# Where the projections of the second layer stand among the attention tiles: four single products, or one block of four and one of two

## The reference

```python
# layer 0
xm = rmsnorm(x) * (1 + scale) + shift          # scale, shift = cond @ w_cond
q, k, v = split(xm @ w_qkv); q, k = rope(q), rope(k)
x = softmax(q k^T / 4) v @ w_out + x
# layer 1
xn = layer_norm(x)
q, k, v = xn @ q_w + q_b, xn @ k_w + k_b, xn @ v_w + v_b
y = softmax(q k^T + mask) v                    # over the keys, no scale
h = layer_norm(y) * (1 + scale) + shift        # scale, shift = silu(cond) @ emb_w + emb_b
x = x + silu(h) @ out_w + out_b
```

## Time and profile before

| | before |
|---|---|
| median of 3 runs | 534.52 us (533.82 to 536.47) |
| the profiled execution: its time / its span | 534.85 / 533.1 us |
| mean granted TensorE clock | 0.994 |
| busy: TensorE matmul / VectorE / ScalarE / POOL | 97% / 78% / 66% / 40% |
| instructions | 9837 |

### The profile page before, as it was taken

One profiled execution on the slowest core, in us unless ns is written; L12 is line 12 of the kernel. 1 busy time (PEld: TensorE's weight loads), 2 busy tenths in 40 slices (PEclk: granted clock), 3 DMA queues, 4 the chain that ended last, 5 costly groups with the idle time before them and its releaser, 6 DMA issues.

```text
span 533.1 us, 9837 instructions
## 1 busy us (share of the span) xinstructions
PE 516.3 (97%) x3342; PEld 195.3 (37%) x3342; DVE 413.7 (78%) x1073; ACT 350.0 (66%) x683; POOL 213.4 (40%) x223
## 2 busy tenths in 40 slices
PE   9978889999999999999999999999999999999987
PEld 5633323243443334332443334332433332332234
DVE  4776588789788678967789677977899998999126
ACT  1542455667767676776768676777788768677961
POOL 3169999238232321823235312723552044004401
PEclk8989999999999999999999999999999999999999
DMA  7982204144134133210331123310331112211011
GB/s 241 344 285 60 81 2 120 40 122 123 39 119 121 41 105 89 86 41 2 119 121 42 40 91 92 99 39 3 120 119 49 54 40 77 67 42 41 2 39 41
DMA packets 43033, 45.25 MB, mean 85 GB/s; under 512 B 4436, under 2 KB 41572, under 8 KB 42600
## 3 DMA queue, kind: packets, MB, share of 16 engines
q1 hardware_dynamic: 42696, 42.79, 26.0%
q10 hardware_dynamic: 288, 1.84, 0.9%
HBM read 25.46 MB, written 18.87 MB: 83 GB/s over the span
## 4 chain that ended last, share of the span: by engine, by line
PE 77%; DVE 14%; DMA 3%; issue 3%; ACT 2%; SPq 1%; DVEq 0%; ACTq 0%
PE bank L502 20%; PE bank L485 13%; PE bank L548 10%; PE bank L465 9%; PE bank L476 9%; DVE masked L818 6%; PE bank L559 5%; PE bank L576 4%; DVE row_max L821 4%; PE bank L517 3%; DMA X<-in_x 3%; PE bank L537 2%; ACT probs L671 1%; PE bank L584 1%; PE bank L615 1%
## 5 line engine op out<-in xcount | busy, mean ns | idle before, releaser
L671 ACT ACTIVATE probs<-bank 128x512 f32<-128x512 f32 x512 | 274.5, 598 | 90.1 <-PE bank L476 89.6
L821 DVE TENSOR_REDUCE row_max<-bank 128x1 f32<-128x512 f32 x256 | 162.6, 684 | 42.0 <-PE bank L485 40.9
L485 PE MATMUL bank<-k_s,q_s 64*128 64x512 f16 x512 | 188.9, 382 | 5.1 <-DVE row_max L821 4.2
L818 DVE CUSTOM_DVE_ANT_0 masked<-bank,mask_bias 128x512 bf16<-128x512 f32 x256 | 163.1, 687 | 18.1 <-PE bank L485 17.5
L465 PE MATMUL bank<-q_s,k_s 64*128 64x512 f16 x512 | 153.2, 381 | 1.1 <-ACT probs L671 0.6
L476 PE MATMUL bank<-shift,kx 64*128 64x512 f16 x512 | 148.5, 376 | 0.9 <-DMA shift<-shift_rows 0.9
L502 PE MATMUL bank<-probs,v_aug 128*17 128x512 f32 x1024 | 134.8, 598 | 0.7 <-ACT probs L671 0.7
L485 PEld LDWEIGHTS bank<-k_s,q_s 64*128 64x128 f16 x512 | 46.9, 93 | 155.0 <-DVE row_max L821 68.0
L548 PE MATMUL bank<-xT,wqkv 128*128 128x512 f32 x128 | 63.5, 628 | 2.8 <-ACT xT L696 2.8
L476 PEld LDWEIGHTS bank<-shift,kx 64*128 64x128 f16 x512 | 45.6, 95 | 28.9 <-DMA shift<-shift_rows 1.4
L465 PEld LDWEIGHTS bank<-q_s,k_s 64*128 64x128 f16 x512 | 31.1, 94 | 15.0 <-ACT probs L671 10.5
(11 more groups left out here) (108 smaller groups left out, 501.9 us busy)
## 6 DMA issues: line engine op xcount, KB each, us to landing
q_parts<-parts SPq DMA_DIRECT2D x64, 128.0 KB
k_parts<-parts SPq DMA_DIRECT2D x64, 128.0 KB
q_s<-q_parts SPq DMA_DIRECT2D x32, 256.0 KB, 2.8
k_s<-k_parts SPq DMA_DIRECT2D x32, 256.0 KB, 3.1
X<-in_x SPq DMA_DIRECT2D x4, 512.0 KB, 7.3
y<-X SPq DMA_DIRECT2D x7, 256.0 KB, 2.2
wc<-in_w_cond ACTq DMA_DIRECT2D x1, 1024.0 KB, 4.9
tables<-in_tables SPq DMA_DIRECT2D x4, 256.0 KB, 7.0
```

Source lines behind the costliest of these rows:

```text
L485: nc.tensor.matmul(bank, m.q_s[slot][rows, i, queries], m.k_s[slot][rows, i, :], start=True, stop=True).then_inc(q.d_made, 1)
L671: act.activation(m.probs[k][:, h, :], bank, ACT.Exp, scale=1.0 if s >= B * NG else float(DH) ** -0.5)\
L818: dve.tensor_tensor_reduce(m.masked[D["max", n, k, h] % ND][:, :], bank, m.mask_bias[:, b, :], 1.0, LOWEST, ALU.add, ALU.max, to)\
L821: dve.tensor_reduce(to, bank, AX.X, ALU.max).then_inc(q.d_done, 1)
```

## The change

The table `PIECES` is changed, and with it the order of POOL's program. The four query and key products of a second-layer batch stand behind tile k = 2 of group 7 + 4b, all four in a row; k = 1 and 3 of that group and k = 0 of the next are left empty. Both value products of a batch stand in a row behind k = 3 of the group where only the second was (9 + 4b, and group 20 for the last batch); the last batch of layer 0 goes the same way, from groups 4 and 5 to group 5. On POOL both value biases of batch b - 1 are added ahead of the splits of batch b, and the one behind the splits is gone; for the last batch both come after its splits. No instruction is added or taken away.

```diff
@@ -93,16 +93,14 @@
     3: ((("embed", 3),), (), (), ()),
-    4: ((), (), (), v(0, 3)[:1]),
 }
 for _b in range(B):
     _s = 5 + NG * _b
 
-    _other = v(0, 3)[1:] if _b == 0 else v(1, _b - 1)[1:]
+    _other = v(0, 3) if _b == 0 else v(1, _b - 1)
     PIECES[_s] = (turn("f0", _b), *one(y(0, _b)), _other)
-    PIECES[_s + 2] = (turn("p1", _b), qk(1, _b, 0), qk(1, _b, 1), qk(1, _b, 2))
-    PIECES[_s + 3] = (qk(1, _b, 3), (), (), v(1, _b)[:1])
-PIECES[20] = (qk(1, LAST, 3), (), v(1, LAST)[:1], v(1, LAST)[1:])
+    PIECES[_s + 2] = (turn("p1", _b), (), qk(1, _b, 0, 1, 2, 3), ())
+PIECES[20] = ((), (), (), v(1, LAST))
@@ -1170,17 +1168,17 @@
-        if b:
-            add_bias(b - 1, 1)
+        for j in range(2 if b else 0):
+            add_bias(b - 1, j)
         for i in range(4):
             split(B + b, i)
-        add_bias(b, 0)
 
     pool.wait_ge(q.late_in, 64)
     modulation()
     for b in range(B):
         project(b)
-    add_bias(LAST, 1)
+    for j in range(2):
+        add_bias(LAST, j)
```

## The result

| | before | after |
|---|---|---|
| median of 20 runs each | 536.27 us (533.81 to 539.45) | 534.06 us (531.68 to 537.52) |
| the profiled execution: its time / its span | 534.85 / 533.1 us | 534.18 / 532.4 us |
| from the value block of group 3, k = 0 to the last one | 401.37 us | 399.29 us |

The ratio is 0.9966 [0.9951, 0.9981]: 0.34% faster, about 1.8 us, between 1.0 and 2.6 (the two medians differ by 2.21). That is less than the 0.5% that the prediction took as the bound of "no change", but clear of zero. The forecast was 0.45%, 2.4 us and a median of 532.1 us.

The account below looks back on a forecast made before the run. TensorE's order was taken as the bound (77% of the chain), VectorE next; query/key -1.72, value -0.83 and long empty runs +0.16 gave -2.4 us, a 532.1 us median. Own range 530.6 to 533.7 us, whole range 529.6 to 536.0.

Parts of the forecast that it names:

- The level: Whole kernel: the median of the runs lies 0.33 us below the profiled execution, giving a forecast median of 532.1 us.
- A: Rival: VectorE's waits do not appear in newly empty tiles, the whole saving stays; -4.8 us, 529.7 us, chance 0.18.
- B: Rival: each product in a row still takes 1.92 us; the sum loses 3.4 us, 535.5 us, chance 0.13.
- The term for k = 1 of group 7 + 4b: This tile, losing its query and key product, goes from 4.56 to 2.82 us: -1.74 us a batch.
- The products in a row: TensorE blocks: 1.72 us a product against 2.00 alone; four take about 7.0 us, their tile 10.0, the value pair 3.7.
- D: Rival: TensorE's clock falls in the block; one block at the lower level adds 6.9 us, 539.0 us, chance 0.03.
- The lengths of the empty tiles: The five tiles behind the block take 2.5, 2.5, 2.8 to 2.9, 3.1 and 2.5 us.
- Rival C: VectorE's time beneath the block is lost and it paces the empty tiles; +5.3 us, 537.4 us, chance 0.08.
- ScalarE ... costed at nothing: At the block, ScalarE's in-order waits and copies add 0 us: no exponentials pending, busy 8.90 of 10.85 us in empty tiles.
- What an empty tile waits for VectorE: In empty tiles, the waits of 0.08, 0.26, 0.24 and 0.08 us (k = 0 to 3) are all VectorE's.
- The late tokens of the last batch: Head of group 22: POOL's normal tokens, delayed by both value biases, still precede TensorE's transposes by 0.8 us.

Follow-up runs that it names:

- half_copy: Changed kernel with ScalarE copying only 64 of 512 columns of the second half of each layer-1 token batch; 530.92 us (one run), steady part 398.23 us.
- light_vector0: Changed kernel with layer 0's row maxima on VectorE reading 384 of 512 columns; 527.77 us (one run), steady part 398.30 us.
- block_k1: Changed kernel with the block of four query and key products behind k = 1 instead of k = 2; 533.54 us, ratio to before 0.9964.
- two_pairs: Changed kernel with the four query and key products as two pairs, behind k = 1 and k = 3; 533.04 us, ratio to before 0.9938.
- early_k3: Changed kernel with token turn and block moved into group 6 + 4b, behind k = 2 and k = 3; 531.82 us, ratio to before 0.9945.
- y_pair: block_k1 with both output products of group 5 + 4b behind k = 1, none behind k = 2; 532.88 us, ratio to before 0.9952.
- pool_delay: Changed kernel with an extra POOL memset of 0.47 us ahead of each layer-1 batch's normal tokens; 533.22 us (one run), steady part 400.45 us.
- turns_k2: Changed kernel with the transpose of the negated maxima behind k = 2 instead of k = 1, from group 4 on; 547.06 us, ratio to before 1.0227.
- turns_k2_ahead: block_k1 with that transpose behind k = 2 and operand loads sent ahead of its wait on the SP queue; 535.30 us, ratio to before 0.9982.

## Where the prediction held and where it failed

The gain is as small as forecast: 0.34% for 0.45%, and in the steady part -2.08 us for -2.4. Two steps failed.

- **The level.** "The median of the runs is 0.33 us below that execution" rested on three runs (534.52). Over 20 runs the kernel before has a median of 536.27, 1.42 us above its profiled execution. So the forecast of 532.1 was 2.0 us too low: the measured 534.06 lies above the forecast's own range of 530.6 to 533.7, though inside the whole one. (Half of A's further saving is 1.2 and half of B's loss 1.7, so that range should have read 530.9 to 533.8.)
- **The term for k = 1 of group 7 + 4b**, with ScalarE costed at nothing: 1.05 us of the gain were lost there, and the prediction came near only since 0.64 us that it did not know of went the other way. That part of its success is luck. Both are told below.

Point by point:

- **The products in a row.** Right. The block took 7.06 us without a wait for a bank and its tile 9.99 (10.0 forecast), the pair 3.65 (3.7). Rival B, 7.7 us a block, falls. The clock was 1.00 in the blocks, so D falls.
- **The lengths of the empty tiles** behind the block. Right to 0.01 to 0.03 us, in layer 1 too (the run in groups 3 and 4 that the prediction called seven empty tiles has six: k = 1 of group 3 to k = 2 of group 4). Rival C needed more than 2.9 on the mean and falls: VectorE's work beneath the block was not lost. The Trainium skill, Perfetto Trace Analysis, Optimization Strategy, says that interleaving regimes may help; this case does not bear it out: taking such an interleaving apart gained 2.08 us of steady part.
- **"ScalarE ... costed at nothing"** failed. The step that read k = 1 of group 7 + 4b as 2.82 took it from a run of empties in which ScalarE had only exponentials. Behind the tile with the token turn it is 3.08: +1.05 us over four batches, and half_copy removes it. The prediction looked at ScalarE's busy share inside the block and inside old empties, not at the one empty tile that follows its longest copy.
- **"What an empty tile waits for VectorE"** failed in half of its parts. Only k = 0 and 3 (0.08 each) are VectorE's alone. The 0.24 of k = 2 is TensorE's own switch, and in k = 1 a second limit stands behind VectorE. It did not spoil the sum, since the sum used lengths and not causes. But it made rival A look possible: of the waits that A would save, light_vector0 freed only 0.09 us in k = 0 and in k = 3 each.
- **The unforecast -0.64 us** came from the meeting of two engines at the end of group 5 + 4b. The prediction changed what stands ahead of POOL's tokens and of k = 3 without asking what else ends there. It hid more than half of the ScalarE miss.
- **The late tokens of the last batch** fit, by 0.57 us where 0.8 was forecast. Timeline of POOL and chain, after:

```profile
387.91 4.84 POOL L791 TENSOR_SCALAR XN<-O,moments_f,rstd_f 128x256 f32<-128x256 f32 x4
```

```profile
393.32 0.59 PE bank L535 x4
```

They end at 392.75 and the transposes start at 393.32, which wait for nothing; 2.7 us in hand have become 0.57.

What stays open: the best version by tile lengths is block_k1, 1.1 us below the change, and its timings (0.9964) cannot be told from the change's (0.9966) nor from two_pairs, early_k3 and y_pair, whose intervals overlap. What of the change of work on TensorE (rows, type) makes a lone product dearer, no run separates. Why the same opening is granted a lower clock in one execution and not in the next was not tried.

## What to carry to other kernels

Price a merge of work by the marginal length of every tile that loses or gains it, and read each empty tile behind its own neighbours: an in-order engine that copies a long operand at the head of one tile is late in the next. Put the block where it covers such lateness. Before giving a stall to one engine, make that engine lighter; two limits that end together hide each other, and a step moved on an in-order queue delays what stands behind it, not what it carries.

## What the runs showed of the hardware

- A lone 128-row float32 product among 64-row float16 work costs 2.00 us and one in a row 1.72 (the tile grew by 5.15 us for three more) to 1.77 (7.06 / 4): about 0.25 us more for standing alone. The output's four transposes lengthen an empty tile by 0.68 us, and a product beside them adds only 1.76.
- POOL's 1.21 us tensor_scalar instructions held VectorE's 0.17 us operations until 0.57 us behind the start: one that began 0.23 us behind it took 0.34 (before), one at 0.11 took 0.47 (pool_delay), and those at 0.53 and 0.74 took 0.17 (after). Beside a tensor_tensor of 0.73 us one took 0.66.
- SyncE waits for the shift's transpose in its program order, so the loads behind that wait went out late with it: 13.7 us in the tiles k = 0 of turns_k2, none in turns_k2_ahead.
- The granted clock stood at 0.62 in 66 to 74 us of one execution, at 1.00 in another of nearly the same code: 1.4 us of a 533 us span, more than most versions here differ by.
